# Every fourth product with B on GpSimd, modulation products in pairs of row strips, and a new hand-written order: a four-layer sequence kernel on one core

## What is computed

```python
# layer 0a: selective scan, INTER = 512 channels, NSTATE = 16 states
dA  = exp(dt[..., None] * A)
dBu = (dt * u)[..., None] * B[:, :, None, :]
s   = dA_t * s + dBu_t                 # along the 512 tokens
y   = einsum('bdn,bn->bd', s, C_t)
# layer 0b: attention, and an MLP whose gate it modulates; R = 16, F = 1024
mod      = 0.1 * tanh(attn @ A)                      # 16 values a token
gate_pre = h @ W_in.T + mod * (h @ A) @ B            # rank-16 term
out      = residual + (silu(gate_pre) * (h @ W_up.T)) @ W_down.T
# layer 1a: gated linear attention in chunks of 64 tokens
# layer 1b: 32 experts, the 4 best of each token, weighted
```

## Time and profile before

| | |
|---|---|
| time, median of 3 runs | 2932.41 us (2931.49 to 2934.28) |
| span of the profiled execution | 2937.5 us |
| PE busy | 2448.7 us, 83% of the span |
| DVE busy | 2137.8 us, 73% |
| ACT busy | 1381.6 us, 47% |
| GpSimd busy | 676.8 us, 23% |

### The profile page before, as it was taken

One profiled execution on the slowest core, in us unless ns is written; L12 is line 12 of the kernel. 1 busy time (PEld: TensorE's weight loads), 2 busy tenths in 40 slices (PEclk: granted clock), 3 DMA queues, 4 the chain that ended last, 5 costly groups with the idle time before them and its releaser, 6 DMA issues.

```text
span 2937.5 us, 36708 instructions
## 1 busy us (share of the span) xinstructions
PE 2448.7 (83%) x12295; PEld 1464.4 (50%) x12295; DVE 2137.8 (73%) x3033; ACT 1381.6 (47%) x2190; POOL 676.8 (23%) x609
## 2 busy tenths in 40 slices
PE   5458888898898888989898989898889797988991
PEld 2335445544554455545544564446444544466880
DVE  4998974798579957994899488948794652246666
ACT  5437254726462646364735474536453326143340
POOL 3012000412140214031303121211420121035661
PEclk8568699969997998799979987899779879998995
DMA  3223220223122311131114211421232073274657
GB/s 133 107 79 103 79 87 20 73 90 113 49 68 79 125 54 60 66 136 64 61 58 139 69 54 58 139 76 46 75 111 71 28 173 124 98 238 138 219 179 304
DMA packets 140453, 297.04 MB, mean 101 GB/s; under 512 B 14416, under 2 KB 83424, under 8 KB 140016
## 3 DMA queue, kind: packets, MB, share of 16 engines
q1 hardware_dynamic: 126448, 256.15, 26.5%
q0 software_dynamic: 13824, 38.55, 3.6%
HBM read 225.11 MB, written 69.54 MB: 100 GB/s over the span
## 4 chain that ended last, share of the span: by engine, by line
PE 45%; DVE 31%; issue 10%; ACT 9%; POOL 3%; DMA 1%; SPq 0%; DVEq 0%; POOLq 0%; ACTq 0%
PE bank L2131 13%; DVE scan L1564 11%; DVE scan L1573 4%; DVE rest L1720 4%; PE bank L2278 4%; PE bank L2294 4%; PE bank L2144 3%; DVE scan L1588 3%; PE bank L2625 3%; PE bank L2333 2%; PE bank L2297 2%; PE bank L2646 2%; PE bank L2118 2%; PE bank L2448 1%; DMA scan<-y_dram 1%
## 5 line engine op out<-in xcount | busy, mean ns | idle before, releaser
L1564 DVE TENSOR_TENSOR_SCAN scan<-scan 128x1024 f32<-128x1024 f32 x256 | 589.7, 2303 | 57.8 <-ACT scan L1286 56.3
L1286 ACT ACTIVATE scan<-scan 128x511 f32<-128x511 f32 x512 | 340.7, 714 | 426.0 <-DVE scan L1564 421.8
L2258 PE MATMUL bank<-ident,scan 128*128 128x128 f32 x2048 | 324.8, 315 | 146.8 <-DVE scan L1573 131.8
L969 POOL DMA_INDIRECT rows_dram<-stage,slot_at x128 | 204.5, 1597 | 989.1 <-DVE scan L1564 496.5
L2258 PEld LDWEIGHTS bank<-ident,scan 128*128 128x128 f32 x2048 | 275.7, 163 | 225.9 <-DVE scan L1573 154.1
L1588 DVE TENSOR_TENSOR scan<-scan 128x1024 f32<-128x1024 f32 x256 | 321.7, 1257 | 13.7 <-PE bank L2258 11.8
L1573 DVE TENSOR_TENSOR scan<-scan 128x1024 f32<-128x1024 f32 x256 | 319.2, 1247 | 0.8 <-DVE xb L1709 0.5
L2333 PE MATMUL bank<-rest 32*128 32x384 f32 (+3 forms) x1024 | 276.9, 652 | 28.9 <-DVE rest L1720 28.4
L1755 DVE TENSOR_TENSOR rest<-rest,bank 128x512 f32<-128x512 f32 x64 | 43.8, 685 | 262.4 <-PE bank L2131 232.6
L1720 DVE TENSOR_REDUCE rest<-bank 128x2 f32<-128x1024 f32 (+3 forms) x176 | 192.9, 1119 | 37.5 <-PE bank L2338 35.6
L1330 ACT ACTIVATE rest<-bank 128x2048 f32<-128x2048 f32 (+3 forms) x128 | 157.9, 1234 | 131.5 <-PE bank L2359 131.4
(11 more groups left out here) (388 smaller groups left out, 4324.4 us busy)
## 6 DMA issues: line engine op xcount, KB each, us to landing
scan<-bc_dram SPq DMA_DIRECT2D x256, 512.0 KB, 3.6
wslot<-wt SPq DMA_DIRECT2D x64, 384.0 KB, 3.0
rows_dram<-scan SPq DMA_DIRECT2D x32, 670.0 KB
scan<-y_dram SPq DMA_DIRECT2D x32, 512.0 KB, 10.2
rest<-rows_dram SPq DMA_DIRECT2D x108, 134.0 KB, 2.7
scan<-rows_dram SPq DMA_DIRECT2D x52, 134.0 KB, 2.9
scan<-wt SPq DMA_DIRECT2D x4, 1536.0 KB, 16.1
wslot<-x SPq DMA_DIRECT2D x8, 512.0 KB, 3.9
```

Source lines behind the costliest of these rows:

```text
L969: g.indirect_dma_start(rows_dram, bass.IndirectOffsetOnAxis(ap=slot_at[:, j:j + 1], axis=0), stage[:, j % NT], None).then_inc(scattered.se ...
L1286: i = a.activation(decay[:, unit % 2, n, 1:], dt[:, c, 1:], ACT.Exp, scale=a_neg[:, c, 2 * pair + n:2 * pair + n + 1])
L1564: d.tensor_tensor_scan(flat, decay[:, unit % 2].rearrange("p n t -> p (n t)"), flat, 0.0, ALU.mult, ALU.add).then_inc(decay_used.sem, 1)
L2258: m = t_.matmul(A.bank(("yT", c))[:, t * P:(t + 1) * P], drive[:, unit % NDRIVE, n, t * P:(t + 1) * P], ident[:, :], is_transpose=True, st ...
```

## The change

It has three parts.

1. With `POOL_EVERY = 4`, `drive` of the units 3, 7, ..., 31 of each turn is made by GpSimd, in a new column `B` of its order. DVE's scan and SP's loads of B wait for GpSimd's own semaphore `drive_pool` where it made the unit.
2. `modb` is laid out in four strips of 32 partitions (16 used in each), by four DMAs in place of one. `mod_w` and `wo_a` hold the 16 weight columns four times, at the strips' places in 128 columns (cleared by GpSimd, copied by DVE in turn 0), so that `gmod` and `tanhT` come out in all four strips. The modulation products of tiles f and f+1 are issued one after the other, from two strips of rows, and the MLP's steps are listed by `mlp_work`.
3. All order strings are drawn anew.

```diff
+STRIPS = 4
+def on_pool(unit):
+    return unit % POOL_EVERY == POOL_EVERY - 1        # POOL_EVERY = 4
 IDLE = {
-    "PE": {"R": 164, "O": 2, "L": 4, "F": 11},
+    "PE": {"R": 168, "O": 2, "L": 4, "F": 11},
...
+def mlp_work():
+    work = [("up", 0), ("gate", 0), ("gate", 1), ("mods", 0), ("up", 1)]
+    for f in range(0, NFT - 2, 2):
+        work += [("down", f), ("gate", f + 2), ("down", f + 1), ("gate", f + 3), ("mods", f + 2), ("up", f + 2), ("up", f + 3)]
+    return work + [("down", NFT - 2), ("down", NFT - 1)]
...
-        modb = sb("modb", FFN, parts=RANK)
+        modb = sb("modb", FFN // STRIPS)
-        wo_a = sb("wo_a", NF * RANK)[:, :].rearrange("p (c r) -> p c r", c=NF)
+        wo_a = sb("wo_a", NF * P)[:, :].rearrange("p (c r) -> p c r", c=NF)
+        mod_w = sb("mod_w", NF * P)[:, :].rearrange("p (c r) -> p c r", c=NF)
-        gmod = area(16, SEQ)[0:RANK, :]
-        tanhT = area(17, SEQ)[0:RANK, :]
+        gmod = area(16, SEQ)
+        tanhT = area(17, SEQ)
...
+            def drive_units(turn):                     # GpSimd, column "B"
+                for unit in range(NU):
+                    load, pair, c = unit_of(unit)
+                    if not on_pool(unit):
+                        continue
+                    yield
+                    pool.wait_ge(bc_in[0][load % 2].sem, bc_in[0][load % 2].at(turn, 16 * (load // 2 + 1)))
+                    steps = fv if c < 2 else uv
+                    pool.wait_ge(steps.sem, steps.named(turn, f"dtu{c}"))
+                    if unit >= NDRIVE or turn:
+                        pool.wait_ge(unit_summed.sem, unit_summed.at(turn, unit - NDRIVE + 1))
+                    apart(pool)
+                    g.tensor_tensor(drive[:, unit % NDRIVE], dtu[:, c].unsqueeze(1).broadcast_to([P, 2, SEQ]), bc[:, load % 2, 0], ALU.mult).then_inc(drive_pool.sem, 1)
...
                     yield                              # DVE, units
-                    dve.wait_ge(drive_ready.sem, drive_ready.at(turn, unit + 1))
+                    if on_pool(unit):
+                        dve.wait_ge(drive_pool.sem, drive_pool.at(turn, made_by_pool(unit + 1)))
+                    else:
+                        dve.wait_ge(drive_ready.sem, drive_ready.at(turn, unit + 1 - made_by_pool(unit + 1)))
...
                     if unit + 1 < NU:
                         yield
-                        drive_unit(turn, unit + 1)
+                        if not on_pool(unit + 1):
+                            drive_unit(turn, unit + 1)
...
+            def mods(turn, first):                     # PE
+                if first == 0:
+                    pe.wait_ge(*B.given_back(turn, ("hA", 0)))
+                for f in (first, first + 1):
+                    rows, g = slice(f % STRIPS * HW, f % STRIPS * HW + RANK), f // STRIPS
+                    m = t_.matmul(B.bank(("gate", f))[:, :], modb[rows, g * P:(g + 1) * P], gmod[rows, :], start=False, stop=True, skip_group_check=True)
+                    filled(B, m)
```

More of the change, by code:

```diff
@@ L99 @@
     "PE": (
[20 rows of a table removed]
[22 rows of a table added]
     ),
     "DVE": (
[20 rows of a table removed]
[22 rows of a table added]
     ),
     "ACT": (
[20 rows of a table removed]
[21 rows of a table added]
     ),
     "POOL": (
-        "U33 R8 X6 R2 X3 R1 X2 R6 X3 U13 R1 X1 U3 X1 R6 X3 U13 R1 X1 U3 X1 R6 X3 U13 R1 X1 U3 X1 R6 X3 U13 R1 "
-        "X1 U3 X1 R6 X3 U13 R1 X1 U3 X1 R6 X5 U14 R1 U2 R6 X30 R1 X19 R4 X5 R1 X4 "
[5 rows of a table added]
     ),
     "SP": (
[3 rows of a table removed]
[4 rows of a table added]
     ),
@@ L193 @@
 NPAIR, NDRIVE = NSTATE // 2, 4
+POOL_EVERY = 4
 NU = NPAIR * NCT
@@ L202, in unit_of, with made_by_pool @@
     return u // 2, u % (2 * NPAIR) // 2, tile
+def on_pool(unit):
+    return unit % POOL_EVERY == POOL_EVERY - 1
+def made_by_pool(units):
+    return sum(1 for unit in range(units) if on_pool(unit))
 def weave(columns, order):
@@ L331 @@
               ("dS", 5), ("AT", 3), ("GO", 1), ("dS", 6), ("GO", 2), ("GO", 3)]
+def mlp_work():
[3 more added lines that the diff above has]
+    return work + [("down", NFT - 2), ("down", NFT - 1)]
+MLP_WORK = mlp_work()
 def rest_jobs():
@@ L340, in rest_jobs @@
     jobs += [("oT", c, "act") for c in range(NF)]
-    jobs += [("hA", 0, "dve"), ("up", 0, "dve"), ("mod", 0, "act"), ("gate", 0, "act")]
-    for f in range(1, NFT):
-        jobs += [("gate", f, "act"), ("up", f, "dve")]
+    jobs += [("hA", 0, "dve"), ("mod", 0, "act")]
+    jobs += [(name, f, "act" if name == "gate" else "dve") for name, f in MLP_WORK if name in ("gate", "up")]
     jobs += [("nT", c, "act") for c in range(NF)]
@@ L681, in build @@
         decay_used = Signal(sem("decay_used"), NU)
-        drive_ready = Signal(sem("drive_ready"), NU)
+        drive_ready = Signal(sem("drive_ready"), NU - made_by_pool(NU))
+        drive_pool = Signal(sem("drive_pool"), made_by_pool(NU))
         unit_done = Signal(sem("unit_done"), NU)
@@ L783, in units_in @@
                     pair, slot = load % NPAIR, load % 2
-                    for g, used in enumerate((drive_ready, unit_done)):
+                    for g in range(2):
                         yield
                         if load >= 2 or turn:
-                            sp.wait_ge(used.sem, used.at(turn, 2 * load - 2))
+                            of, used = (turn, 2 * load - 2) if load else (turn - 1, NU - 2)
+                            if g == 0 and used:
+                                sp.wait_ge(drive_ready.sem, drive_ready.at(of, used - made_by_pool(used)))
+                                if made_by_pool(used) or of:
+                                    sp.wait_ge(drive_pool.sem, drive_pool.at(of, made_by_pool(used)))
+                            elif g == 0:
+                                sp.wait_ge(drive_ready.sem, drive_ready.at(of, 0))
+                                sp.wait_ge(drive_pool.sem, drive_pool.at(of, 0))
+                            else:
+                                sp.wait_ge(unit_done.sem, unit_done.at(of, used))
                         sp.dma_start(bc[:, slot, g], rows[g, 2 * pair:2 * pair + 2, :].partition_broadcast(P)).then_inc(bc_in[g][slot].sem, 16)
@@ L899, in _ @@
             sp.dma_start(res[:, begin:], w[:, begin:]).then_inc(weights_in, 16)
-            sp.dma_start(modb[:, :], mod_b).then_inc(weights_in, 16)
+            for s in range(STRIPS):
+                sp.dma_start(modb[s * HW:s * HW + RANK, :].rearrange("p (g n) -> p g n", n=P),
+                             mod_b.rearrange("r (g s n) -> s r g n", s=STRIPS, n=P)[s]).then_inc(weights_in, 16)
             sp.dma_start(gk2, g_gk2).then_inc(weights_in, 16)
@@ L1097, in other_constants @@
                 const(g.memset(decay_all[:, 0:4 * SEQ:SEQ], 0.0))
+                const(g.memset(mod_w, 0.0))
+                const(g.memset(wo_a, 0.0))
                 pool.sem_inc(cleared.sem, 1)
@@ L1123, in _ @@
                 "U": itertools.chain.from_iterable(late_part(turn - 2 if turn >= 2 else None, turn) for turn in range(BATCH)),
+                "B": itertools.chain.from_iterable(drive_units(turn) for turn in range(BATCH)),
                 "R": itertools.chain(idle(IDLE["POOL"]["R"]), *(rest_part(turn) for turn in range(BATCH)), tail_part(BATCH - 1)),
@@ L1188, in front_part @@
                 if turn == 0:
-                    act.wait_ge(weights_in, 16 * (4 + P // GV))
+                    act.wait_ge(weights_in, 16 * (3 + STRIPS + P // GV))
                 for c in range(NCT):
@@ L1230, in front_part @@
                 if turn == 0:
-                    act.wait_ge(wo_steps, 3)
+                    act.wait_ge(wo_steps, 4)
                     a.activation(g_gkw.rearrange("p c n -> p (c n)"), bank[4][:, 0:NF * GHK], ACT.Copy).then_inc(prep, 1)
@@ L1340, in rest_part @@
                 yield
-                empty(B, turn, ("mod", 0), tanhT, ACT.Tanh, src=lambda b: b[0:RANK, :])
+                empty(B, turn, ("mod", 0), tanhT, ACT.Tanh)
                 yield
@@ L1480, in bc2, with in_strips, four_times @@
                 return ap.unsqueeze(2).broadcast_to([P, ap.shape[1], n])
+            def in_strips(ap):
+                return ap.rearrange("p c (s r) -> p c s r", s=STRIPS)[:, :, :, 0:RANK]
+            def four_times(ap):
+                return ap.unsqueeze(2).broadcast_to([P, NF, STRIPS, RANK])
             def norm_stats(steps, turn, src, st, mv_, off_, name):
@@ L1511, in front_part @@
                     dve.wait_ge(wo_steps, 1)
-                    d.tensor_copy(wo_a, bank[2][:, 0:NF * RANK].rearrange("p (c r) -> p c r", c=NF)).then_inc(wo_steps, 1)
+                    d.tensor_copy(in_strips(mod_w), four_times(mod_a)).then_inc(wo_steps, 1)
+                    d.tensor_copy(in_strips(wo_a), four_times(bank[2][:, 0:NF * RANK].rearrange("p (c r) -> p c r", c=NF))).then_inc(wo_steps, 1)
                 yield
@@ L1744, in rest_part @@
                 dve.wait_ge(B.ready.sem, B.filled_at(turn, ("hA", 0)))
```

(42 more changed lines are left out.)

## The result

| kernel | median, us | ratio to the kernel before |
|---|---|---|
| before | 2932.20 (2931.49 to 2934.28) | |
| changed | 2997.86 (2993.09 to 3005.97) | 1.0222 (95%: 1.0205 to 1.0238) |

What follows compares the result with a forecast made beforehand. PE was taken to bound the MLP, DVE the score and probability stages, both in part behind the MLP. Terms -33 + 7 + 7 + 7 + 23 - 21 = -10 took 2932.4 to 2922 us; range 2868 to 2976.

Steps and rivals of the forecast that it cites:

- Part 1: MLP on PE: 32 pairs of modulation products overlap in two strips of rows, saving 1.03 us each, -33 us.
- Parts 2, 3 and 6: Unit sums moved into the MLP on PE, +7; new MLP waits, +7; DVE work relieved behind the MLP, -21.
- part 6: Behind the MLP: earlier units move DVE work into the MLP, shortening the stretch by 3 us a turn, -21 us.
- part 3: MLP: new waits ahead of down(0), behind a 2.8 us chain, and for weight tiles; +1 a turn, +7 us.
- Part 4: GpSimd's queue: a turn's last product stands ahead of the norm's root, costing +1 a turn, +7 us.
- Part 5: Shared SBUF port: GpSimd products hold DVE in ramp and probability stage, score stage 0; +23 us, bounds -37 to +70.
- Rival 2: GpSimd's in-order queue becomes the bound: scatters stretch, products come late, DVE idles; +42, 2974 us, chance 0.22.
- Rival 1: The port hardly costs: GpSimd's products fall beside reductions and waits, relieving DVE; -60, 2872 us, chance 0.22.
- Rival 3: MLP: the paired modulation products do not overlap, so their saving is 0; 2955 us, chance 0.06.

Runs made afterwards that it cites:

- e10: e6 with both modulation products of each pair fed from one strip of rows, so that they cannot overlap: 2912.74 us.
- e6: Changed kernel with all products with B back on DVE and the late scatters ahead of the norm's root: 2880.63 us, ratio 0.9811.
- e1: Changed kernel with all 256 products with B back on DVE, pairs and new order kept: 2931.65 us, ratio 0.9988.
- e3: Kernel before with the paired modulation products alone, old order strings, the MLP's PE steps regrouped: 2970.87 us, ratio 1.0127.
- e7: e2's order with only the products of units 27 and 31 (16 products) on GpSimd: 2891.49 us.
- e8: e2's order with only the products of units 7, 11, 15 and 19 (32 products) on GpSimd: 2937.17 us.
- e9: e6 with GpSimd making e8's 32 products a second time, into a tile nobody reads; DVE keeps all its own: 2943.43 us.
- e11: e6 with the products of units 7, 11, 15 and 19 (32 products) made by nobody, waits kept: 2865.42 us.
- e2: Changed kernel with the late scatters moved ahead of the norm's root, products still on GpSimd: 2975.95 us, ratio 1.0137.

## Why the prediction was wrong, by its own steps

The chain of medians from before to changed adds up step by step: the new order with mended scatters -22 (e10), pairs -32 (e6), late scatters +51 (e1), products +66: +63. The first group of runs has +66, where the kernel before read 2 to 4 us lower than in the later groups.

- **Part 1 was right in its mechanism, and partly lucky in its number:** -33 forecast, -32.1 measured from e10 to e6, -20 in the changed kernel. The profile shows what was foretold: four 16-row records, the next product 1.06 us after their start. But e10's serial pair takes 1.91 us, so from e10 to e6 a pair can save 0.85 us, 27 in all. The MLPs, where all of it was to lie, get 23 us shorter there; another 9 come from behind them.
- **Parts 2, 3 and 6** forecast +7, +7 and -21, -7 in sum; e10 has -22 for all of them. They were not told apart by a run. By stages of the trace, e10 against the kernel before has +5 in the score stages, +13 in the probability stages, for which the prediction has no term, -1 in the MLPs, -2 in the holes behind them, -31 in the linear attention, where part 6 looked for it, and -9 in ramp and tail. The wait ahead of down(0) does not show on PE in turn 2, where two unit sums fill that gap; e3, with nothing in a like gap, has it at 2.8 us a turn, the size of part 3's chain.
- **Part 4 is the step that failed first.** It charged one thing to GpSimd's queue, B31 ahead of the norm's root (+7; e7 has 11 for that and more). It did not follow the scatters, though the order printed ahead of the prediction reads `rs0 #B3 x x #sc11 ... #sc15 memset x`: the last five scatters of a turn, once done before the next turn's memset and root of the routed rows' norm came up, now stand just ahead of both. Asking who waits for each would have led from `t_rs` to ACT, from ACT to DVE's `xb`, and to a hole in a stage that DVE bounds, behind which PE runs at half its clock. That is +51 with the products on DVE, and +22 with them on GpSimd: the two losses cover one another in part.
- **Part 5 had the mechanism and missed the size,** +23 against +66, or +95 with the queue mended. The hold was right where it falls: 2.13 us forecast, 2.1 on the stretched rows of e8, and 1.5 us of longer DVE time as the mean of e9's products. Wrong were three terms. The saving was put at 1.12 us where DVE sets the pace; e11 shows 0.48, since ACT and PE are close behind a DVE that is busy 97% of a stage. The products in the score and probability stages were put at 25, of which 14 were charged; in the changed kernel 34 start there. And the score stage was put at 0, for its reductions read PSUM; but its scan operations do not, and from e6 to e2 the score stages of turns 1 to 5 grow by 6.5 us on average and the probability stages by 4.8. The upper bound of 70, made of holds with no saving, was nearer to the truth than the value taken.
- **Rival 2 had the place right,** GpSimd's in-order queue with stretched scatters, but the wrong victim: it has DVE waiting for products. In the changed kernel DVE's waits have no line for a late product; it waits for ACT, which waits for the queue. **Rival 1** falls with e9. **Rival 3** falls with e10. The prediction also has no term for PE's clock: the mean granted clock is 0.871 in e6's profiled run, 0.862 in e1's and 0.850 in the changed kernel's.

The Trainium skill, page "SBUF — State Buffer", section "Who interferes with whom", says that whichever engine issues first keeps the shared ports for its whole instruction and the other one blocks. e8's rows agree: 3.31 in place of 1.20 us, and 4.90 in place of 2.34 for GpSimd's product.

## What to carry to other kernels

Moving work to an idle engine pays only by what the busy one gives back on the path, and that is to be priced against the engine that is next (here 0.48 of 1.12 us); what the move costs by contention comes on top (here 1.96 us beside a DVE that sets the pace, 0.7 at the MLP and behind it). When an in-order queue is drawn anew, follow every instruction that is moved past another one to whoever waits at the end of the chain, the small ones too: five to nine late scatters in each of four turns, in the queue of a 1 us root, cost more than the paired products gained. An idle hole can cost more than its length, for here PE came out of it at half its clock. Two small products in separate strips of rows took the time of one (1.06 us, against 1.91 in one strip), wherever their weights were there in time.

## What the runs showed of the hardware

An indirect scatter took GpSimd 0.96 us at the end of the linear attention and 1.8 to 2.9 us beside a dense scan. The first row is from GpSimd's timeline in e6, the second from that of the changed kernel just ahead of the score stage. That DVE's work stretches it was not tested by itself.

```profile
1123.43 0.96 POOL L1012 DMA_INDIRECT rows_dram<-stage,slot_at  x1 [0.30 <-issue]
```

```profile
1216.69 2.86 POOL L1015 DMA_INDIRECT rows_dram<-stage,slot_at  x1 [0.30 <-issue]
```

A GpSimd product of 1024 columns took 2.34 us undisturbed, less than twice a 512-column one (2 x 1.27), and 4.90 in the row of e8 beside DVE (the longest of that run 6.5).

PE's clock fell in the hole of the changed kernel's turn 3: granted 1.00 ahead of 7 us of idle time and 0.50 behind it, and the same 16 records took 1.16 us, then 2.08. In e1's turn 2 it went from 1.00 to 0.50 over an idle time of 8.0 us. Idle time is not the only way to this level: in e6's turn 2 the granted clock is 0.50 from 897 on, with no such hole ahead of it.
